# Scan stage with convolution products of two taps, a second copy of the padded input, and new half-slot tables

## What is computed

```python
xn = layernorm(x)
# s: Mamba block, forward and backward over l, on the same xz
x, z = split(xz, 2)                                  # 512 channels each
x = silu(depthwise_conv(x, conv_w, 4 taps, padded left by 3) + conv_b)
x_dbl = x @ Wx.T
dt = softplus(x_dbl[..., :64] @ Wdt.T + bdt); B, C = 16 columns each
h_t = exp(dt_t * A) * h_(t-1) + dt_t * B_t * x_t     # 512 channels x 16 states
y_t = sum_n h_t[n] * C_t[n] + x_t * D;  y * silu(z) -> out projection
# g: mixture of 8 experts, top 2, hidden 512;  x = x + s * silu(g)
```

## Time and profile before

| | before |
|---|---|
| median of 3 executions | 3241.3 us (3237.01 to 3243.83) |
| profiled execution | 3248.7 us, its span 3246.9 us |
| busy share of TensorE, VectorE, ScalarE, GpSimd | 84%, 69%, 54%, 54% |
| mean granted clock of TensorE | 0.914 of full speed |
| forward units 2 to 14 | 128.0 to 131.3 us each (first scan to first scan) |
| unit 0, unit 15 | 134, 110 us |

### The profile page before, as it was taken

How to read it: one execution, slowest core, us unless ns; L and a number is a source line. 1 busy time by engine, 2 the same in 40 slices (tenths; PEclk the granted TensorE clock), 3 DMA queues, 4 the chain that set the end, 5 groups by cost and what they waited for, 6 DMA issues and landing times. The chain is left out here.

```text
span 3246.9 us, 40447 instructions
## 1 busy us (share of the span) xinstructions
PE 2737.8 (84%) x13486; PEld 1826.9 (56%) x13486; DVE 2252.4 (69%) x2812; ACT 1765.3 (54%) x2691; POOL 1754.2 (54%) x554
## 2 busy tenths in 40 slices
PE   5466887887888888878968878777999999999999
PEld 5134665665666565666656656555455555555554
DVE  5287989889889989989988988984442442442430
ACT  1355767758848758758758767641332332322322
POOL 0598868878878878778778887861000000000000
PEclk9777898899999989989989989887999999999999
DMA  6222324333333334333333332323000000000000
GB/s 254 85 69 94 119 101 140 108 109 119 123 106 121 107 104 147 109 105 117 129 115 115 111 134 90 130 89 131 26 33 0 32 32 0 32 18 15 6 7 7
DMA packets 149278, 283.24 MB, mean 87 GB/s; under 512 B 23659, under 2 KB 97878, under 8 KB 149078
## 3 DMA queue, kind: packets, MB, share of 16 engines
q1 hardware_dynamic: 142934, 264.08, 23.8%
q0 software_dynamic: 6144, 16.79, 1.5%
HBM read 239.13 MB, written 41.68 MB: 86 GB/s over the span
## 5 line engine op out<-in xcount | busy, mean ns | idle before, releaser
L708 POOL TENSOR_TENSOR hs<-u,bb 128x2048 f32<-128x2048 f32 x256 | 1159.3, 4534 | 368.5 <-PE hT L1013 323.3
L884 DVE TENSOR_TENSOR_SCAN hs<-dA,hs 128x1024 f32<-128x1024 f32 x512 | 1166.3, 2284 | 122.7 <-POOL hs L708 75.9
L797 ACT ACTIVATE dA<-dt,cols 128x511 f32<-128x511 f32 x1024 | 661.8, 680 | 412.9 <-DVE hs L884 408.6
L1013 PE MATMUL hT<-ident,hs 128*128 128x128 f32 x3584 | 558.4, 297 | 264.2 <-DVE held L894 222.4
L1013 PEld LDWEIGHTS hT<-ident,hs 128*128 128x128 f32 x3584 | 434.9, 151 | 405.6 <-DVE held L894 290.2
L894 DVE SCALAR_TENSOR_TENSOR held<-hT,ct,held 128x512 f32<-128x512 f32 x864 | 603.8, 742 | 54.2 <-PE hT L1013 53.1
L1287 ACT ACTIVATE gl<-bank,cols_sb 128x512 f32<-128x512 f32 x192 | 130.7, 687 | 528.4 <-PE bank L1526 528.1
L1526 PE MATMUL bank<-mT,cms_sb 128*128 128x512 f32 x768 | 363.6, 598 | 10.1 <-ACT mT L1281 8.6
L1032 PE MATMUL moe<-xgT,held 128*128 128x128 f32 x2400 | 334.4, 299 | 30.0 <-ACT xgT L811 28.2
L1032 PEld LDWEIGHTS moe<-xgT,held 128*128 128x128 f32 x2400 | 321.3, 214 | 61.4 <-ACT xgT L811 37.6
L136 POOL COPY cur<-slot 128x8 uint32 (+1 forms) x8 | 1.5, 187 | 640.9 <-DVE held L148 631.3
(11 more groups left out here) (219 smaller groups left out, 3332.1 us busy)
## 6 DMA issues: line engine op xcount, KB each, us to landing
held<-wl SPq DMA_DIRECT2D x75, 1024.0 KB
bb<-b_scratch SPq DMA_DIRECT2D x128, 512.0 KB, 5.6
held<-wl SPq DMA_DIRECT2D x75, 512.0 KB
xg_scratch<-zero SPq DMA_DIRECT2D x10, 960.0 KB, 5.4
xg<-xg_scratch SPq DMA_DIRECT2D x75, 128.0 KB
yg_scratch<-yg SPq DMA_DIRECT2D x75, 128.0 KB, 1.7
held<-x SPq DMA_DIRECT2D x16, 512.0 KB, 8.7
cb<-b_scratch SPq DMA_DIRECT2D x32, 256.0 KB, 4.7
```

What stands on the lines that cost most here:

```text
L708: nc.gpsimd.tensor_tensor(hs[n % HS][:, :, :], u[d][:, :, :], row, ALU.mult).then_inc(dBu_ready, 1)
L797: last = nc.scalar.activation(dst, src, ACT.Exp, scale=cols[:, at:at + 1])
L884: nc.vector.tensor_tensor_scan(h, decay, h, 0.0, ALU.mult, ALU.add).then_inc(scan_done, 1)
L1013: last = nc.tensor.transpose(hT[c % 2][:, k * P:(k + 1) * P], hs[n % HS][:, k, c * P:(c + 1) * P], ident[:, :])
```

## The change

Two copies of the padded input are kept. Copy g holds channels of half g (64 partitions) as they are, and in its other 64 partitions the same channels one position earlier. So one matmul over 128 partitions applies two taps to 64 channels, and writes 64 partitions; a product is two of them for each half. `w_tap` holds the tap columns for both arrangements, loaded by four more transfers; the 64 diagonal blocks of `taps` are 64 by 64. ScalarE writes both copies straight from the bank, four activations where one was. The tables of preparation, tiles, skips, softplus quarters (`SOFT`) and GpSimd's weighings (`WEIGH`, `ADD`) are new; `FIN` only writes out what was there. At the half slots in `LATE` ScalarE's decay comes behind the preparation and tile pieces. The diff, without its unchanged lines:

```diff
+HP = P // 2
...
+        w_tap = s0("w_tap", [P, 2, CB])
...
-        N_W = 6
+        N_W = 10
...
+                for g in range(2):
+                    for half in range(2):
+                        sp.dma_start(w_tap[HP * half:HP * (half + 1), g, :], cols0[HP * g:HP * (g + 1), CW:CB]).then_inc(w_sem, 16)
...
-            xpad = s0("xpad", [P, DB, L + 2 * (KC - 1)])
...
+            xpad = [s0(f"xpad{g}", [P, DB, L + 2 * (KC - 1)]) for g in range(2)]
...
-            taps = s0("taps", [P, 2 * DB * KC, P])
+            taps = s0("taps", [P, 2, DB, 2, KC // 2, HP])
...
-            plan(0, "proj", (0, 1, 6, 7))
-            plan(0, "conv", (2, 4, 8, 10))
+            plan(0, "proj", (0, 1, 4, 7))
+            plan(0, "conv", (3, 6, 8, 10))
...
-            plan(0, "dt", (13, 14, 16, 17))
-            plan(0, "soft", (17,))
-            plan(0, "c", (21,))
-            plan(1, "gate", (20, 22, 24, 25))
+            plan(0, "dt", (14, 16, 18, 20))
+            plan(0, "soft", (21,))
+            plan(0, "c", (16,))
+            plan(1, "gate", (20, 21, 22, 24))
...
-            plan(1, "soft", (15,))
-            plan(1, "c", (16,))
+            plan(1, "soft", (16,))
+            plan(1, "c", (17,))
...
-            SKIP = (0, 1, 4, 5)
+            SKIP = (0, 2, 3, 4)
...
+            SOFT = ((13, 14, 15, 15), (15, 15, 15, 15))
...
+            LATE = ((3, 6, 15, 19, 21, 23, 28), (3, 5, 6, 16, 17, 18, 19, 20, 21, 22, 25, 28, 30))
+            FIN = (0, 0, 1, 1)
+            WEIGH, ADD = ((1, 2), (2, 2)), ((3, 3), (3, 3))
...
+            def pair_at(d, q):
...
+                return 2 * q if d == 0 else 2 * (KC - 1) - 1 - 2 * q
...
+            def tap_of(d, q, early):
...
+                return pair_at(d, q) + early if d == 0 else 2 * (KC - 1) - pair_at(d, q) - early
...
+            TILE_AT = ((0, 6, 12, 19, 25), (0, 6, 12, 19, 25))
...
-                every = 5 if last and d == 1 else 6
+                starts = range(0, 5 * T0, 5) if last and d == 1 else TILE_AT[d]
...
-                        out[every * (i % T0) + at].append((piece, i))
+                        out[starts[i % T0] + at].append((piece, i))
...
-                            if n - 2 in POOLN:
-                                weigh(d, unit, POOLN.index(n - 2))
-                            if n - 3 in POOLN:
-                                add(d, unit, b, POOLN.index(n - 3))
+                            for k, m in enumerate(POOLN):
+                                if n == m + WEIGH[d][k]:
+                                    weigh(d, unit, k)
+                                if n == m + ADD[d][k]:
+                                    add(d, unit, b, k)
...
-                            if n >= NS - 3 and more:
-                                for quarter in ((0,), (1,), (2, 3))[n - (NS - 3)]:
+                            for quarter in range(4) if more else ():
+                                if n == SOFT[d][quarter]:
...
-                        nc.scalar.activation(xpad[:, k, KC - 1:KC - 1 + L], src[:, :], ACT.Copy).then_inc(p_used, 1)
+                        for g in range(2):
+                            own, other = slice(HP * g, HP * (g + 1)), slice(HP * (1 - g), HP * (2 - g))
+                            nc.scalar.activation(xpad[g][own, k, KC - 1:KC - 1 + L], src[own, :], ACT.Copy)
+                            last = nc.scalar.activation(xpad[g][other, k, KC - 2:KC - 2 + L], src[own, :], ACT.Copy)
+                        last.then_inc(p_used, 1)
...
-                                if n + 3 < NS:
-                                    decay(d, unit, n + 3, j)
-                                elif more:
-                                    decay(1 - d, unit + 1, n + 3 - NS, j)
+                                if s not in LATE[d]:
+                                    if n + 3 < NS:
+                                        decay(d, unit, n + 3, j)
+                                    elif more:
+                                        decay(1 - d, unit + 1, n + 3 - NS, j)
...
+                                if s in LATE[d]:
+                                    if n + 3 < NS:
+                                        decay(d, unit, n + 3, j)
+                                    elif more:
+                                        decay(1 - d, unit + 1, n + 3 - NS, j)
...
-                nc.vector.memset(xpad[:, :, 0:KC - 1], 0.0).then_inc(hT_used, 1)
-                nc.vector.memset(xpad[:, :, KC - 1 + L:], 0.0).then_inc(hT_used, 1)
+                for g in range(2):
+                    nc.vector.memset(xpad[g][:, :, :], 0.0).then_inc(hT_used, 1)
...
-                for i in range(2 * DB * KC):
-                    nc.vector.tensor_scalar(taps[:, i, :], ident[:, :], cols[:, CW + i:CW + i + 1], None, ALU.mult).then_inc(taps_ready, 1)
+                for d in range(2):
+                    for k in range(DB):
+                        for g in range(2):
+                            for q in range(KC // 2):
+                                for half in range(2):
+                                    rows_ = slice(HP * half, HP * (half + 1))
+                                    at = (d * DB + k) * KC + tap_of(d, q, int(half != g))
+                                    nc.vector.tensor_scalar(taps[rows_, d, k, g, q, :], ident[rows_, rows_], w_tap[rows_, g, at:at + 1],
+                                                            None, ALU.mult).then_inc(taps_ready, 1)
...
-                                if n == 0 and d == 0 and later(b):
-                                    for k in (2 * j, 2 * j + 1):
+                                for k in range(DB) if d == 0 and later(b) else ():
+                                    if FIN[k] == 2 * n + j:
...
-                            pe.wait_ge(taps_ready, 2 * DB * KC)
-                        for t in range(KC):
-                            at = t if d == 0 else 2 * (KC - 1) - t
-                            last = mm(dst[:, :], taps[:, (d * DB + k) * KC + t, :], xpad[:, k, at:at + L], start=(t == 0), stop=(t == KC - 1))
+                            pe.wait_ge(taps_ready, 4 * DB * KC)
+                        for q in range(KC // 2):
+                            at = pair_at(d, q)
+                            for g in range(2):
+                                last = mm(dst[HP * g:HP * (g + 1), :], taps[:, d, k, g, q, :], xpad[g][:, k, at:at + L],
+                                          start=(q == 0), stop=(q == KC // 2 - 1))
```

## The result

The changed kernel takes 3223.3 us (median of 5 executions, 3220.5 to 3225.7), the kernel before 3241.3 in the same comparison: a ratio of 0.9945, 95% interval 0.9931 to 0.9960. It is faster by 18 us, where 39 were forecast. The direction was right and the time lies in the range; the size was not.

A forecast was written before the change was run, and what follows sets the result against it. VectorE sets the scan stage's pace, TensorE a close second. Gains of 2.8 + 1.8 + 1.4 = 6.0 us per batch, times 7, are 42; 3241.3 - 42 + 3 for the start = 3202 us, range 3168 to 3250.

The forecast's parts named there:

- Part 6: Start, until the first convolution: two memsets and 64 half-height tap instructions; net +3 us (0 to +9).
- Part 1: Convolution product with two taps per matmul: 3.6 to 2.3 us, 1.3 saved (0 to 1.7); by itself costed at 0.
- Part 2: Both copies by ScalarE, backward unit: 6.6 us more work, costing nothing since VectorE waits 0.74 us at slot 8 anyway.
- Part 3: Forward unit, first half: weighing ahead of product 4 cuts the 3.85 us wait before slot 8 to 0.2; net 2.8 us.
- Part 4: Forward unit, second half: moved softplus, gates, tiles and later decays remove waits; gain capped by GpSimd at 1.8 us.
- Part 5: Backward unit, second half: dt and softplus moved to other slots; gain capped by GpSimd at 1.4 us.
- Rival (c): Copies lie on the path in slots 0 to 8 of the backward unit; slower by 17 us, 3258; chance 0.14.
- rival (b): 10 of the 16.2 us per batch won, turns coming earlier and GpSimd's caps loosening; 3174 us; chance 0.12.
- (a): Halves of the convolution do not overlap, a product stays 3.6 us; kernel 3220 us; chance 0.10.
- (d): No change: softplus quarters behind product 15 make the next product 4.6 us late, eating the forward gain; 3244; chance 0.12.
- signs of being wrong: Backward-unit decay waits in slots 2 to 9, over 1 us for GpSimd at slot 28, or a 3.6 us convolution.

The follow-up runs named there:

- e2: Changed kernel with its 64 tap instructions reordered, all of the lower 64 partitions first, then all of the upper; one execution, 3186.3 us, not compared with other times.
- e8: Changed kernel with the loops over q and g exchanged, so the two matmuls of a half follow one another; ratio 0.9923 to the kernel before.
- e3: New convolution (two taps per product) and ScalarE's copies with all tables of the kernel before; ratio 1.0109 to the kernel before.
- e4: New tables with the convolution of the kernel before (4 taps, one copy, its start); ratio 0.9948 to the kernel before.
- e7: Changed kernel with a faster start, and two 128-partition activations per proj piece instead of four half-height ones (convolution's result differs); ratio 0.9845 to the kernel before.
- e6: Changed kernel with a faster start, and GpSimd's weighing in forward units set back behind product 4; ratio 0.9917 to the kernel before.
- e10: Changed kernel with a faster start, GpSimd adding the backward unit's x*D behind product 2 of the next unit; 3167.7 us, kernel before 3225.6, ratio 0.9826.

## Why the prediction was wrong in size

**Part 6, the start, is the step that failed.** It took a tap instruction of 64 by 64 at 0.13 us, with bounds 0.10 and 0.21 from larger instructions on all partitions, and came to +3 us with 0 to +9. Measured were 0.32 us each and +17.2 us (+14.3 without the stall). Until the first convolution +5.2 us were forecast, and +18.1 came (93.26 to 111.32). The memsets were right (1.84 forecast, 1.78 each). The bound was drawn from instructions that all use the same partitions; those here alternate between two halves, and e2 shows that this alone nearly doubles the price. Set in with 20.35 for the 8.3 us of taps, the start is 3 + 12 = +15, and the forecast would have been 3214 instead of 3202. The 9 us from there to 3223 are those by which the medians differ less than the profiles; their cause stays open.

**Part 1**, right in kind, mis-sized: 1.7 us saved per product, the bound, not 1.3. The reading behind the 1.3, by which records overlap only between neighbours on different halves, is refuted by e8: without such neighbours a product should have taken some 2.8 us and took 1.95. The switch between widths costs what was read from L1434, 0.1 us each way: the first record starts 203 ns behind the turn before it for 109 in the kernel before, and what follows starts 522 ns behind the last record for 431. So the net saving for TensorE is 1.5 us per product. That the shorter product is worth nothing by itself and that parts 2 and 3 would come out later without it, e3 and e4 bear out: it wins 22.8 us in the forward units on top of the tables. The prediction gave no price for that.

**Part 2** was costed at 0 net, since VectorE would wait 0.74 us for GpSimd at slot 8 anyway. The turns of slot 2 are late by 1.5 us (1.4 forecast) and decay 2 by 0.35 (0.3); but slot 10 adds 0.56, which the working did not reach, and the copies are 0.59 and not 0.55. The cover was worth 0.63, and e7 puts the rest at 1.9 us per unit, 13 in all, where the sum had 0. It doesn't show in the total, because the forward units won 11 us more than forecast.

**Part 3** came out in number, and that was in part luck. The waits of slots 2 to 15 fell by 2.7 us on average over the seven units (4.35 to 1.66), 2.8 forecast. But the wait before slot 8 fell by 2.2 (3.86 to 1.66) and not to 0.2, since GpSimd's product 6 came 0.4 us later in the unit than worked and VectorE was there 1.0 sooner. 0.5 us of small waits in slots 6 and 7 went, which the working did not count. And the late silu, put at 0.8, cost nothing: no wait stands at slot 11. The weighing, which the working had in front, is worth 0.7 of it by e6, and by e4 there is no gain in these slots at all without the short product.

**Part 4**: the waits of slots 16 to 31 fell by 1.8 us (3.5 to 1.7), 1.8 forecast; the stretch became 2.0 shorter. Another 1.2 came off slots 0 and 1, where the working had said that the change leaves both waits, and slots 2 to 15 became 3.0 shorter. That is why the forward units won 6.2 each and not 4.6.

**Part 5**: the cap by GpSimd was seen in the right place, and product 13 ends 82.2 us into the unit (81.7 before). But 1.4 us were to be won up to slot 28, and none was: it starts 106.1 us into unit 7 in both kernels, since GpSimd's chain came 0.5 late out of the first half, waited 0.6 for a turn before product 15 and 0.3 after the softplus. The 0.35 us per backward unit in the table come from behind slot 28. e10 shows that it was a cap: with one addition less in that stretch the waits go.

Rival (c), copies on the path, has happened in part, and rival (b), more won in the forward unit, too; they nearly cancelled in the scan stage. Neither (a) nor (d) was seen: at slot 28, for the product behind the softplus quarters, VectorE waited 0.24 us on average in forward and 1.1 in backward units, not 4.6. Of the signs of being wrong that the prediction named, two did come in backward units, waits for decays in slots 2 to 9 (0.35 us on average) and more than 1 us for GpSimd at slot 28.

## What to carry to other kernels

Cost the code ahead of a loop by its own instructions as carefully as the loop: work that runs once took back more than a third of what seven batches had won (17.2 of 45.7 us). When a wait is explained by an engine's chain, find the member of the chain that itself waits (here, by the trace, the add that waits for the skip): taking the weighing out of its way won only 0.7 us. Price work against the wait that it would uncover next, and take work out of the chain only where the engine idles later (the late sum). And price a table of slots together with the work that it is made for: the convolution alone was slower than before, while on top of its tables it won 22.8 us in the forward units.

## What was not expected of the hardware

**Alternating partition halves.** VectorE instructions of 64 partitions by 64 columns start 0.17 us apart on average when successive ones use the same half, and 0.32 apart when they alternate between partitions 0 to 63 and 64 to 127 (10.76 and 20.35 us for 64).

**Changing between 128 and 64 columns of weights** costs TensorE 0.09 us each way (from one start to the next, medians of 38 places each: 203 for 109 ns ahead of a product that follows a turn, 522 for 431 behind one), the same in e8.

**A half-height activation is no cheaper**: 0.59 us for 64x512, 0.60 for 128x512.

**Narrow float32 matmuls.** The records of a convolution product start in pairs, 7 ns apart within a pair and 431 ns from pair to pair, and in e8, where neighbours use the same 64 columns of weights, likewise (13 and 431 ns).
**A stall of ScalarE** of 14 to 29 us in all in the prologue, in all six profiles of two groups and in none of the eight of the two others, with either kernel.
